# LayerNorms inside the sublayers' blocks, merged row scaling in a recurrence, and a two-table sum in PSUM

## The reference, cut to what matters

```
def _layernorm(x, axis=-1, eps=1e-05):
    m = jnp.mean(x, axis=axis, keepdims=True)
    v = jnp.var(x, axis=axis, keepdims=True)
    return (x - m) / jnp.sqrt(v + eps)
...
x = x + L0_xattn(_layernorm(x), ctx); x = x + L0_attn(_layernorm(x)); x = x + L0_ffn(_layernorm(x))
x = x + L1_xattn(_layernorm(x), ctx); x = x + L1_attn(_layernorm(x)); x = x + L1_ffn(_layernorm(x))
x = x + L2_xattn(_layernorm(x), ctx); x = x + L2_attn(_layernorm(x)); x = x + L2_ffn(_layernorm(x))
x = x + L3_xattn(_layernorm(x), ctx); x = x + L3_attn(_layernorm(x)); x = x + L3_ffn(_layernorm(x))
```

```
def step(carry, inp):
    S, R = carry
    ...
    S = a_t[..., None] * S
    kp = jnp.einsum('bhd,bhde->bhe', kn, S)
    S = S + b_t[..., None, None] * kn[..., None] * (v_t - kp)[..., None, :]
    o = jnp.einsum('bhji,bhj->bhi', S, q_t)
    ... the same for R, with r = clip(v_t - pred, -1, 1)
```

```
topk_weight, topk_idx = jax.lax.top_k(scores, C)          # scores [16, 2048], C = 256
xg = flat_x[topk_idx]
...
h = jax.nn.gelu(g, approximate=False) * u
eo = jnp.einsum('eci,edi->ecd', h, Wd) * topk_weight[..., None]
flat_out = jnp.zeros_like(flat_x).at[topk_idx.reshape(-1)].add(eo.reshape(-1, d))
return flat_out + shared
```

## Time and profile before

| | us |
|---|---|
| median of three runs | 3391.75 |
| lowest, highest | 3390.59, 3400.45 |
| the profiled execution | 3403.23 |
| its span in the profile | 3401.4 |
| stage of l0_xattn | 0 to 164.07 |
| stage of l1_xattn | 491.15 to 981.19 |
| stage of l1_attn | 981.19 to 2158.01 |
| stage of l2_ffn | 2860.53 to 3104.31 |
| stage of l3_ffn | 3263.41 to 3401.4 |

### The profile page before, as it was taken

How to read it: one execution, slowest core, us unless ns; L and a number is a source line. 1 busy time by engine, 2 the same in 40 slices (tenths; PEclk the granted TensorE clock), 3 DMA queues, 4 the chain that set the end, 5 groups by cost and what they waited for, 6 DMA issues and landing times. The chain is left out here.

```text
span 3401.4 us, 114629 instructions
## 1 busy us (share of the span) xinstructions
PE 2751.1 (81%) x49147; PEld 1976.2 (58%) x49147; DVE 2186.5 (64%) x5679; ACT 1449.1 (43%) x3334; POOL 549.9 (16%) x578
## 2 busy tenths in 40 slices
PE   8977478999966688888888887479998998697754
PEld 5644464444435566776767665356665666375633
DVE  3346425655556989888999885357776664664751
ACT  4342233333333445444545444256666334363410
POOL 0000334555510000000000000000001331062024
PEclk9878688999978898989999998779998998796865
DMA  2200331111110000000000000000001001252013
GB/s 82 63 1 1 104 123 48 47 41 41 41 48 3 4 4 4 4 4 4 4 4 4 4 4 3 2 20 25 24 24 44 1 1 38 71 130 66 5 43 102
DMA packets 69048, 109.26 MB, mean 32 GB/s; under 512 B 10240, under 2 KB 54929, under 8 KB 67761
## 3 DMA queue, kind: packets, MB, share of 16 engines
q1 hardware_dynamic: 56912, 80.34, 7.7%
q0 software_dynamic: 11696, 22.40, 2.6%
HBM read 90.06 MB, written 16.51 MB: 31 GB/s over the span
## 5 line engine op out<-in xcount | busy, mean ns | idle before, releaser
L2914 PE MATMUL psum<-l1d_rw,l1d_cols 64*32 64x32 f32 (+2 forms) x20480 | 240.8, 216 | 86.0 <-issue 63.3
L2914 PEld LDWEIGHTS psum<-l1d_rw,l1d_cols 64*32 64x32 f32 x20480 | 209.5, 108 | 129.5 <-issue 102.5
L2412 POOL TENSOR_TENSOR l2x_qx<-l2x_q,consts 128x128 f32<-128x128 f32 x64 | 25.6, 400 | 1598.7 <-DVE l2x_q L2583 1275.8
L2337 POOL TENSOR_SCALAR l1xs_p<-l1xs_p,l1xs_col 128x257 f32<-128x257 f32 x256 | 238.5, 934 | 243.2 <-DVE l1xs_col L2300 242.7
L2265 ACT ACTIVATE l1xs_p<-psum,l1xs_col 128x257 f32<-128x257 f32 x256 | 122.2, 478 | 256.0 <-DVE l1xs_col L2295 255.8
L2295 DVE TENSOR_REDUCE l1xs_col<-psum 128x1 f32<-128x257 f32 x256 | 107.4, 419 | 138.4 <-PE psum L2217 138.4
L3163 DVE TENSOR_TENSOR l1d_rw<-l1d_rw,l1d_tots 128x512 f32<-128x512 f32 x240 | 153.1, 688 | 56.5 <-PE psum L2914 55.2
L2701 ACT COPY l1d_ya<-psum 128x512 f32<-128x512 f32 x160 | 93.0, 590 | 192.6 <-PE psum L2954 191.4
L2217 PE MATMUL psum<-l1xs_keys,l1xs_qx 128*32 128x257 f32 x2048 | 161.0, 394 | 4.1 <-ACT l1xs_p L2265 4.1
L2229 PE MATMUL psum<-l1xs_pt,l1xs_vals 32*128 32x512 f32 x1152 | 162.0, 637 | 1.3 <-DVE l1xs_pt L2307 1.3
L2855 PE MATMUL psum<-l1d_src,l1d_wp 128*128 128x128 f32 x1024 | 136.4, 289 | 15.8 <-ACT l1d_src L2706 14.5
(11 more groups left out here) (566 smaller groups left out, 6941.2 us busy)
## 6 DMA issues: line engine op xcount, KB each, us to landing
l2f_w<-in_l2f_w SPq DMA_DIRECT2D x16, 768.0 KB
l1xs_vals<-in_ctx_strips SPq DMA_DIRECT2D x16, 576.0 KB
l0x_ctxT<-in_ctxT SPq DMA_DIRECT2D x16, 516.0 KB, 3.7
l1xs_keys<-in_ctxT SPq DMA_DIRECT2D x16, 516.0 KB
l2x_ctxT<-in_ctxT SPq DMA_DIRECT2D x64, 129.0 KB, 2.1
l1d_wp<-in_l1d_wp SPq DMA_DIRECT2D x1, 2048.0 KB, 8.1
l2f_acc<-l2f_zero SPq DMA_DIRECT2D x8, 256.0 KB, 4.3
l2f_sums<-l2f_acc SPq DMA_DIRECT2D x8, 256.0 KB, 5.0
```

The lines of the kernel that those rows point to most:

```text
L2337: nc.gpsimd.tensor_scalar(p[:, t % 4, :S2], p[:, t % 4, :S2], col[:, 2, t % 4:t % 4 + 1], None, ALU.mult).then_inc(s["norm"], 1)
L2914: mm = nc.tensor.matmul(k.ps[bank0 + pr + e // per * 2][b * T:b * T + T, e % per * w:(e % per + 1) * w], cols[rr, 2 * n, e * 128 + b * T:e ...
```

## The change

- `load_state`, `layer_norm`, `end_load` and `add_normed` go. A class `Norm` has the same instructions, as parts that each sublayer puts at the head of its own Block on each engine. The sublayer's body then waits per chunk for `done` where it can work by chunks (`ready`), or for the last chunk, and each engine waits for the weights behind its part of the norm (`loaded`).
- `Norm` uses four PSUM banks (a `base` of 0 or 4) instead of eight: the chunks turned back go to the banks of the rows, the last one to the bank of chunk 0 behind its copy. ACT's order has the copy of chunk 0 ahead of root 3 and normalise 2.
- In the first sublayer the constants are loaded first, then x in four DMAs of 256 KB, and PE waits for each chunk. The last sublayer stores x in four DMAs, each behind its chunk's last add.
- The DMAs of the weights of `l2_xattn` and `l2_ffn` are issued while their norm runs.
- `l1_attn`: both norms are in the sublayer's Block, the second following the first chunk by chunk; X += XN moves to POOL in four instructions; `rw` becomes [128, 7, 32, T], and `advance` scales its two or three features in one instruction.
- `l1_xattn`: the second product leaves PSUM on DVE instead of ACT.
- `l2_ffn`: SP loads table 0 when its last rows are in, then table 1 when its are. PE adds both into PSUM by matmuls with the identity, the first table starting and the second adding; DVE's sum goes.

```
+    def tensor(self, pe):
...
+        for c in range(NCH):
+            if c < NCH - 1:
+                pe.wait_ge(s["early"], c + 1)
+            else:
+                pe.wait_ge(s["done"], 1)
...
+        normalise(1)
+        out(0)
+        root(3)
+        normalise(2)
+        out(1)
...
@@ routed_experts
+            if last:
+                for c in range(NCH):
+                    sp.wait_ge(s["x"], c + 1)
+                    sp.dma_start(k.out[:, c * CH:(c + 1) * CH], k.X[:, c * CH:(c + 1) * CH]).then_inc(stored, 16)
...
             for t in range(NT):
+                if t % PER == 0:
+                    norm.ready(pe, t // PER)
...
@@ l2_ffn
             for j in range(2):
                 sp.wait_ge(put[j], 16 * e)
-            for c in range(NCH):
-                for j in range(2):
+                for c in range(NCH):
                     sp.dma_start(sums[:, j, c * 4:(c + 1) * 4, :],
                                  acc[j][c * CH:(c + 1) * CH, :].rearrange("(t p) d -> p t d", p=128)
-                                 ).then_inc(back[c], 16)
+                                 ).then_inc(back[j][c], 16)
...
-            for c in range(NCH):
-                pe.wait_ge(s["sums"], c + 1)
-                for t in range(4 * c, 4 * c + 4):
-                    mm = nc.tensor.transpose(k.ps[c][:, (t % 4) * 128:(t % 4 + 1) * 128], sums[:, 0, t, :],
-                                             k.const("ident"))
-                mm.then_inc(s["turn_mm"], 1)
+            for j in range(2):
+                for c in range(NCH):
+                    pe.wait_ge(back[j][c], 16)
+                    for t in range(4 * c, 4 * c + 4):
+                        mm = nc.tensor.matmul(k.ps[c][:, (t % 4) * 128:(t % 4 + 1) * 128], sums[:, j, t, :],
+                                              k.const("ident"), start=(j == 0 and t % 4 == 0),
+                                              stop=(j == 1 and t % 4 == 3))
+                    if j == 1:
+                        mm.then_inc(s["turn_mm"], 1)
...
-                dve.wait_ge(back[c], 32)
-                nc.vector.tensor_tensor(sums[:, 0, c * 4:(c + 1) * 4, :], sums[:, 0, c * 4:(c + 1) * 4, :],
-                                        sums[:, 1, c * 4:(c + 1) * 4, :], ALU.add).then_inc(s["sums"], 1)
...
@@ l1_attn
+        first = Norm(k, ph, affine, base=4)
+        norm = Norm(k, ph, weights, src=k.XN, affine=(lncol[:, 0:1], lncol[:, 1:2]), bufs=first.bufs, behind=first,
+                    free=s["resid"])
...
-        rw = sb("rw", [128, 32, 7, T])
+        rw = sb("rw", [128, 7, 32, T])
...
+                nc.gpsimd.tensor_tensor(x, x, k.XN[:, c * CH:(c + 1) * CH], ALU.add).then_inc(s["resid"], 1)
...
-                for f in feats:
-                    x = half(rw[:, :, f, :], lv, 1)
-                    tt(x, x, total(n, gate, lv, 0).to_broadcast(wide), ALU.mult)
+                x = (rw[:, feats].rearrange("p f g (n two m) -> p f (g n) two m", two=2, m=m)[:, :, :, 1, :])
+                over = total(n, gate, lv, 0).rearrange("p g n o -> p (g n) o").unsqueeze(1)
+                tt(x, x, over.to_broadcast([128, feats.stop - feats.start, 32 * (16 >> lv), m]), ALU.mult)
...
@@ program
-        load_state(k)
+        k.arrivals = arriving(k)
         for p in PHASES:
             before = nc.snapshot_sems()
-            sublayer = SUBLAYERS[p](k)
-            layer_norm(k, k.X, k.XN, weights=next(sublayer))
-            for _ in sublayer:
-                pass
+            SUBLAYERS[p](k)
             nc.clear_and_free_semaphores(nc.allocated_since(before))
             nc.all_engine_barrier()
-        store_state(k)
+        if not k.stored:
+            store_state(k)
```

More of the change, by code:

```diff
@@ L114, in const, with arriving @@
         return self.c[:rows, o:o + w]
[L117 to L126, removed]
+def arriving(k):
+    return k.sem("consts_in"), [k.sem(f"state_in{c}") for c in range(NCH)]
 def store_state(k):
@@ L416, in loads @@
     return k.sem(nm + "loaded"), pairs
-def end_load(k, weights):
-    loaded, pairs = weights
-    with k.nc.Block() as block:
-        @block.sync
-        def _(sp):
-            sp.wait_ge(loaded, 16 * len(pairs))
 def l0_attn(k):
@@ L906, with routed_experts @@
 NT = N // 128
-def add_normed(k, nm):
-    nc, done = k.nc, k.sem(nm + "residual")
-    with nc.Block() as block:
-        @block.vector
-        def _(dve):
-            nc.vector.tensor_tensor(k.X[:], k.X[:], k.XN[:], ALU.add).then_inc(done, 1)
-            dve.wait_ge(done, 1)
-def routed_experts(k, nm, e, f4, gated):
+def routed_experts(k, nm, e, f4, gated, last=False):
     nc, ph, cap = k.nc, ExitStack(), 256
@@ L1052, in _ @@
         def _(act):
+            norm.scalar(act)
             if gated:
@@ L1205, in _ @@
         def _(pool):
+            norm.loaded(pool)
             def weights(j):
@@ L1258, in l2_ffn @@
     put = [k.sem(f"l2f_put{j}") for j in range(2)]
-    back = [k.sem(f"l2f_back{j}") for j in range(NCH)]
+    back = [[k.sem(f"l2f_back{j}{c}") for c in range(NCH)] for j in range(2)]
     tab = nc.dram_tensor("l2f_tab", (N, row), F32, kind="Internal").ap()
@@ L2649, in l1_attn @@
              "u", "p_mm", "r", "y2_mm", "y2", "z2_mm", "t2", "wr_mm", "wr", "o_mm", "o", "out_mm", "x", "zero", "diag",
-             "norm", "turn", "steps", "colr", "kr")
+             "norm", "turn", "steps", "resid", "colr", "kr")
     s = {n: k.sem("l1d_" + n) for n in names}
@@ L2691, in l1_attn, with _ @@
         turned = (6, 7, 4, 5)
+        @block.sync
+        def _(sp):
+            first.sync(sp)
+            norm.sync(sp)
+        @block.gpsimd
+        def _(pool):
+            for c in range(NCH):
+                first.ready(pool, c)
+                x = k.X[:, c * CH:(c + 1) * CH]
+                nc.gpsimd.tensor_tensor(x, x, k.XN[:, c * CH:(c + 1) * CH], ALU.add).then_inc(s["resid"], 1)
         @block.scalar
         def _(act):
+            first.scalar(act)
+            norm.scalar(act)
+            norm.ready(act, NCH - 1)
             copy, activation = nc.scalar.copy, nc.scalar.activation
@@ L2849, in _ @@
         def _(pe):
+            first.tensor(pe)
+            norm.tensor(pe)
+            norm.ready(pe, NCH - 1)
             def projected(i, n, name, done):
@@ L3108, in _ @@
         def _(dve):
+            first.vector(dve)
+            norm.vector(dve)
             tt, vc = nc.vector.tensor_tensor, nc.vector
```

340 lines of the change are left out of this document (209 added, 131 removed).

## The result

The changed kernel takes 3360.64 us (median of 6 runs, 3354.01 to 3374.3) where the kernel before takes 3391.84 (6 runs, 3380.91 to 3400.51): 0.9901 of the time, interval 0.9874 to 0.9927. That is 31.2 us less, and the forecast was 3361. The interval is some 9 us wide on either side, so the total hitting the forecast says little about the terms; the rows do.

What follows compares the result with a forecast made beforehand. No engine was taken as full (PE busy 81%), so savings count only at the wait that ends last in a stage. Ten terms sum to 30.5 us off 3403.23, scaled by 0.9966 to 3361; range 3346 to 3377.

Steps and rivals of the forecast that it cites:

- 1, start: First sublayer's loads: constants first and x in quarters let PE start near 5.0 instead of 7.32; 2.3 us.
- 2, seven entries: Seven plain sublayers: PE's 1.31 us idle between norm and body goes, less 0.5 for ACT's slip; 0.8 each, 5.6 us.
- 3, l1_xattn: Weight products of l1_xattn are one run of PE, so who empties PSUM matters little; 0 us.
- 4, head of l1_attn: Ahead of l1_attn's loop: second norm follows the first by chunks, adds hidden on POOL, memsets start earlier; 6.9 us.
- 5, loop: l1_attn's loop: merged advances save DVE 14.1 us, but only that behind its last wait for PE counts; 1.2 us.
- Rival C: Idle at a Block's start is each engine's price for new code, so entries give nothing; 3374 us, chance 0.19.
- B: l1_attn's loop is bound by DVE, so all 14.1 us saved there count; 3348 us, chance 0.12.
- D: PE's fills in l1_attn slow down reading `rw` at 4 KB strides; 3402 us and up, chance 0.06.
- E: Fills slow by about 10% (24 us), or as much is lost elsewhere in l1_attn's loop; 3385 us, chance 0.08.
- 6, 7, 8: Entries of l1_ffn (DVE starts earlier), l2_xattn and l2_ffn (weight loads land during the norm); 2.4, 3.9 and 3.4 us.
- 9, tail: End of l2_ffn: early load of table 0 and PE's identity products bring the last X add earlier; 2.0 us, ends 0.5 and 5.
- 10, end: Kernel's final store in quarters: the last 256 KB lands in 4.3 us, at 3398.1 against 3401.05; 2.8 us.

Runs made afterwards that it cites:

- l1a_late_work: Changed kernel with l1_attn alone, plus a spare 128 x 1024 VectorE memset in each block behind the last advance of R; median 1207.59 us.
- l3f_after: Changed kernel with l3_ffn as its only sublayer, the other eleven left out; median 136.76 us.
- l3f_before: Kernel before the change with l3_ffn as its only sublayer, the other eleven left out; median 141.70 us.
- l1a_before: Kernel before the change with l1_attn as its only sublayer, the other eleven left out; median 1199.92 us.
- l2xf_after: Changed kernel with l2_xattn and l2_ffn only, the other ten sublayers left out; median 626.91 us.
- l2xf_old_tail: Changed kernel with l2_xattn and l2_ffn only, but both tables loaded pair by pair behind the last scatter, summed on VectorE and turned; median 630.48 us.

## Why the prediction was right, term by term

The direction, the size and the mechanism that carries most of it (idle time at the seams goes) held. That the sum came out is luck in part: errors of both signs met. By step:

- **1, start: 2.3, measured 0.5** (18.55 to 18.02 for the norm's last copy; 0 to 1.1 over the other kernels), of which the slip of ACT's copies, counted in step 2, hides 0.5. The term was mis-sized: I took the constants and one quarter as what is waited for, but the norm's end hangs on the later quarters, and PE still waited for one until 7.46, where all of x and the constants had been there at 7.32 before.
- **2, seven entries: 5.6, measured about 2.** In l0_xattn the first product came 2.05 earlier, 1.5 more than step 1 has. PE's first product came 1.03 earlier in l0_attn, l0_ffn, l3_attn and l3_ffn, and 1.05 in l2_attn counted from the norm's first turn back (6.46 to 5.41; the turns ahead ran at a lower clock before), a little more than the 0.8. What failed is the claim that only this matters. Where ScalarE's first function waits, the table's load of 1.28 now stands behind the wait (l0_ffn, l3_attn, l3_ffn), and those bodies reach that function 0.2 to 0.3 later than before. That this is a loss is shown for l3_ffn alone. In l3_attn PE's first product with l3a_phi still came 0.85 earlier (17.38 to 16.53 into the stage), in part because the 16 products ahead took 2.08 where they had taken 3.17. In l3_xattn PE now waits 1.72 for the last weight load, and counted as in l2_attn its first product came 0.85 later (6.49 to 7.34). That leaves 1.5 in l0_xattn and 1.0 each in l0_attn and l2_attn, less 0.85 and, counted at ScalarE's first function, 0.6. Rival C had nothing from the entries for another reason: the idle time did go, but another wait took its place in three or four of the seven.

  The Trainium skill, page "ScalarE activation tables: per-element evaluation and per-set limits", section "Table sets in the compiler and the runtime", says that the back end places table loads per block. The rows agree with that: the load stood at the Block's start before and right ahead of its first use in the merged one. The page does not say what this costs where the use waits; the row of the load before would have been the place to ask, and I did not.
- **3, l1_xattn: 0.** 490.04 and 490.00.
- **4, head of l1_attn: 6.9, measured 6.1** in the full kernel. The adds on POOL are hidden, as said. Alone the stage gained 7.0, of which the same copy's place gives 6.7 (46.84 to 40.16) with the start in it.
- **5, loop: 1.2, measured 0 within some 8 us.** DVE saved 13 where 14.1 was forecast, and gave 11.7 of it back in its waits for PE's fills, about half of them at the last advance of R that was named. By the formula of the Trainium skill, page "VectorE: DVE Perf Modes", section "The TRN2 errata — SBUF-src ops pay a fixed extra latency per instruction", the saving would have been 30, an estimate; each merged row fits the formula (1.757 and 1.226 measured, 1.757 and 1.224 by it), but the separate ones overlap. Rivals B, D and E are out: the loop is not bound by DVE as a whole, and the layout costs nothing that can be seen. That all work behind the last wait is on the path is not shown: `l1a_late_work` cost something, but not clearly its full price.
- **6, 7, 8: 2.4, 3.9, 3.4, measured 2.8, 4.1, 3.7** (stage of l1_ffn 58.20 to 55.44; first products). Right.
- **9, tail: 2.0, measured 3.6 to 5.5.** Mis-sized: PE's products ran at 0.12 for an instruction, not 0.22 (32 of them in 3.89 at 3074.26), and kept up with the loads. I took the slow end because PE had next to nothing to do while the last scatters ran, but the change itself gives it the products of table 0 there, and the granted clock was 1.00 behind them. The upper bound of 5 was the right case.
- **10, end: 2.8, measured 4.3.** The 256 KB store lands in about 2.0 (DMA view of `l3f_after`), not in 4.3: that row was a median over eight writes issued one behind the other, behind four loads. The 1 MB store is not one figure either: it took 6.3 in the kernel before, 5.4 in `l3f_before` and 3.9 in `l1a_before`.

The measured terms make 0.5 + 2.1 + 0 + 6.1 + 0 + 2.8 + 4.1 + 3.7 + 4.3 (tail) + 4.3 (end) = 27.9, where the timed difference is 31.2 with about 9 either way. So the terms agree with the time but do not close on it, and the profiles show what they leave out. In l3_ffn the last add of X came 4.6 earlier in the stage (130.30 to 125.66), though the exponential came 0.2 later; alone, from `l3f_before` to `l3f_after`, that add came 0.9 earlier and the exponential 0.3. The 4.8 between the two in the full kernel is in no term, and its cause is open. l0_attn's stage, 2.2 longer in one profile and 0.2 shorter in the other, is not explained beyond the clock.

## What to carry to other kernels

Ask of each saving which wait follows it on its engine: in one loop 13 us taken off VectorE, most of it ahead of its waits for TensorE, gave nothing that could be measured, and 11.7 of them came back as idle time. When two Blocks become one, look for what the boundary had done early for free; here it was a table load of 1.28 us on ScalarE, and one dummy activation ahead of the wait gets it back. And never credit a change with the difference of two stage lengths from one profile each: the same code differed by 8.9 us in 164, at mean granted clocks of 0.90 and 0.96.

## What the runs showed of the hardware that was not expected

- A merged fp32 tensor_tensor of 128 x 1536 took 1.757 us and three of 128 x 512 back to back 1.90: instructions that follow each other overlap, so merging saves 0.07 for each one that goes.
- The granted clock in the same stretch of the same code was 0.89 in one execution and 1.00 in another, and five runs of one sublayer of 1193 us spread over 17 us, where those of one of 142 us spread over 1.4.
- Where TensorE was given the products of table 0 during the last scatters, the ones behind them had a granted clock of 1.00 (32 instructions in 4.10 us of `l2xf_after`); without them the turns at that place ran at 0.50 (16 in 4.46 of `l2xf_old_tail`).
- Four stores of 256 KB issued one behind the other, each behind a VectorE add, landed in 2.0 us each by the median (DMA view of `l3f_after`), where one of 1 MB took 5.4 in `l3f_before` (and 3.9 in `l1a_before`, for a reason that no run shows):

```profile
out_xT<-X SPq DMA_DIRECT2D x4, 256.0 KB, 2.0
```

```profile
out_xT<-X SPq DMA_DIRECT2D x1, 1024.0 KB, 5.4
```
